# Reordering the prologue of a cross-attention and feed-forward kernel: Q first, batch 0's Q spread without DRAM, later batches prepared one step sooner

## The reference, cut to what matters

```python
Q = heads(layernorm(x) @ w_q.T)        # x: 8 batches x 256 tokens x 128
K = heads(ctx @ w_k.T); V = heads(ctx @ w_v.T)   # 16 heads of width 8
attn = softmax(where(mask, Q @ K.T / sqrt(8), -inf))
x = x + (attn @ V) @ w_o.T
h = silu(layernorm(x) @ w_gate.T) * (layernorm(x) @ w_up.T)    # 384 wide
out = x + h @ w_down.T
```

## Time and profile before

| | |
|---|---|
| median of 3 executions | 182.03 us (181.5 to 182.88) |
| the profiled execution's own time | 182.24 us |
| its span in the trace | 180.4 us |
| prologue, up to the first score matmul | 19.62 us |
| sixteen maxima of batch 0 | 13.03 us |
| steps 0 to 6 | 15.55, 15.67, 16.56, 17.20, 17.19, 16.67, 16.67 us |
| step 7 and the end | 32.24 us |

### The profile page before, as it was taken

The page is one execution under the profiler, slowest core; times in us unless marked ns, Lnnn a source line. Parts: engine busy times, 40 slices in busy tenths (PEclk is TensorE's granted clock), DMA queues, the critical chain, the costliest instruction groups (busy, mean ns, idle before and its releaser), DMA issues.

```text
span 180.4 us, 4294 instructions
## 1 busy us (share of the span) xinstructions
PE 165.1 (91%) x1630; PEld 103.6 (57%) x1630; DVE 134.4 (74%) x315; ACT 109.9 (61%) x231; POOL 63.4 (35%) x108
## 2 busy tenths in 40 slices
PE   5877999998998799999999999999899999999693
PEld 5556655554554346557655765575465546656583
DVE  6844579789499779868986889789978982533763
ACT  4434421985596588847866786677677746866130
POOL 8421655531307741971396058100500050000100
PEclk9996999999999999999999999999999999999999
DMA  4729989188059007803950593069100000100011
GB/s 150 270 64 204 243 144 239 52 219 140 0 145 202 11 8 216 136 0 93 222 79 0 143 198 47 4 187 174 25 2 29 5 0 2 33 2 0 4 60 29
DMA packets 17525, 17.06 MB, mean 95 GB/s; under 512 B 1536, under 2 KB 16128, under 8 KB 16832
## 3 DMA queue, kind: packets, MB, share of 16 engines
q1 hardware_dynamic: 17040, 16.12, 39.0%
q10 hardware_dynamic: 464, 0.67, 1.4%
HBM read 9.24 MB, written 7.34 MB: 92 GB/s over the span
## 4 chain that ended last, share of the span: by engine, by line
PE 68%; DVE 22%; ACT 2%; DMA 2%; issue 2%; ACTq 1%; SPq 1%
PE pv_bank L340 14%; DVE neg_max L818 12%; PE score_bank L280 11%; PE max_bank L297 5%; PE pv_bank L428 5%; PE ffn_bank L405 4%; PE ffn_bank L393 4%; PE ffn_bank L396 3%; PE post_bank L381 2%; DMA ctx_all<-ctxT 2%; PE prep_bank L319 2%; PE post_bank L357 2%; DVE x L896 2%; DVE stats L902 2%; PE prep_bank L311 2%
## 5 line engine op out<-in xcount | busy, mean ns | idle before, releaser
L818 DVE TENSOR_REDUCE neg_max<-max_bank 128x2 f32<-128x512 f32 x128 | 82.0, 684 | 15.6 <-PE max_bank L297 15.2
L613 ACT ACTIVATE probs<-score_bank 128x512 f32<-128x512 f32 x128 | 70.3, 598 | 22.0 <-PE score_bank L280 21.8
L297 PE MATMUL max_bank<-k_ops,q_ops 49*128 49x256 bf16 x256 | 43.2, 273 | 4.0 <-DVE neg_max L818 3.9
L280 PE MATMUL score_bank<-q_ops,k_ops 51*128 51x256 bf16 x256 | 42.8, 273 | 0.6 <-ACT probs L613 0.4
L340 PE MATMUL pv_bank<-probs,v_ops 128*32 128x256 f32 x480 | 32.5, 385 | 0.0
L280 PEld LDWEIGHTS score_bank<-q_ops,k_ops 51*128 51x128 bf16 x256 | 19.3, 94 | 19.5 <-ACT probs L613 9.1
L297 PEld LDWEIGHTS max_bank<-k_ops,q_ops 49*128 49x128 bf16 x256 | 16.7, 94 | 10.9 <-DVE neg_max L818 7.5
L1101 POOL CAST max_parts<-neg_max 128x16 bf16<-128x16 f32 x14 | 2.8, 198 | 54.9 <-DVE neg_max L818 54.9
L340 PEld LDWEIGHTS pv_bank<-probs,v_ops 128*32 128x32 f32 x480 | 13.7, 109 | 9.5 <-issue 4.0
L1108 POOL TENSOR_TENSOR rstd<-var,minus_half 128x2 f32<-128x2 f32 x8 | 5.6, 702 | 32.5 <-DVE var L915 32.5
L428 PE MATMUL pv_bank<-ident_bf 128*128 128x128 bf16 x150 | 14.7, 252 | 1.9 <-POOL ident_bf L1131 1.9
(11 more groups left out here) (139 smaller groups left out, 232.3 us busy)
## 6 DMA issues: line engine op xcount, KB each, us to landing
k_ops<-k_rows SPq DMA_DIRECT2D x7, 384.0 KB, 4.7
q_ops<-q_rows SPq DMA_DIRECT2D x7, 384.0 KB, 6.2
k_rows<-kq_parts SPq DMA_DIRECT2D x8, 192.0 KB, 2.1
q_rows<-kq_parts SPq DMA_DIRECT2D x8, 192.0 KB, 2.2
k_rows<-kq_parts SPq DMA_DIRECT2D x8, 128.0 KB, 2.1
q_rows<-kq_parts SPq DMA_DIRECT2D x8, 128.0 KB, 2.1
out<-y SPq DMA_DIRECT2D x7, 128.0 KB, 2.3
x_all<-x SPq DMA_DIRECT2D x1, 768.0 KB, 6.2
```

What stands on the lines that cost most here:

```text
L280: mm = pe.matmul(score_bank[k % 2][:, t * S:(t + 1) * S], rows(k_ops, b, ROWS)[:, k, t * P:(t + 1) * P], rows(q_ops, b, ROWS)[:, k, :], st ...
L297: mm = pe.matmul(max_bank[k % 2][:, t * S:(t + 1) * S], rows(q_ops, b, MAX_ROWS)[:, k, t * P:(t + 1) * P], rows(k_ops, b, MAX_ROWS)[:, k, ...
L613: act.activation(probs[:, k % RING].rearrange("p t s -> p (t s)"), score_bank[k % 2][:, :], ACT.Exp, scale=SCALE).then_inc(probs_ready, 1)
L818: dve.tensor_reduce(neg_max[:, b % 2, :, k], max_bank[k % 2][:, :].rearrange("p (t s) -> p t s", t=TT), AX.X, ALU.max, negate=True).then_i ...
```

## The change

1. SP's loads: x of batch 0 before ctx of batch 0; x in three more pieces (batch 1, batches 2 and 3, batches 4 to 7), the last issued only after batch 1's K and mask; ctx of batches 2 and 3 with the first loads.
2. Q's chain of batch 0 is moved ahead on PE, ACT and DVE. The fill of the second Q buffer leaves DVE, that of the second K buffer moves back on ACT, behind the prologue; the fills of the V buffers 2 and 3 go from ACT to POOL; the mask is made earlier.
3. Batch 0's Q no longer goes through DRAM: six DMAs, five on SP and one on ACT, copy a part of 128 partitions straight into a block of 8 rows by 16 heads (`spread_q`).
4. K of batch 1 is read back before the last write of batch 1's Q.
5. The preparation (x's statistics, layer norm, K and Q) of batches 4 to 7 is one step sooner, in steps 0 to 3. Steps 0 to 2 have one batch's statistics each and the stage of the sixteen maxima has batch 4's.
6. The numbers of `keep_warm` are changed, and four of the seven in step 0 are gone, two halved.

```diff
-        q_rows = [nc.dram_tensor(f"q_rows{b}", [SPREAD, HEADS * S], BF16, kind="Internal") for b in range(B)]
+        q_rows = {b: nc.dram_tensor(f"q_rows{b}", [SPREAD, HEADS * S], BF16, kind="Internal") for b in range(1, B)}
...
+        def spread_q(eng, part, n):
+
+            first, stride, _ = Q_GROUPS[part]
+            row = DK * (first + stride * n)
+            eng.dma_start(rows(q_ops, 0, SPREAD)[row:row + DK], kq_parts[:, 0, part, S:2 * S]).then_inc(q_direct, 16)
...
+            sp.dma_start(x_all[:, 0], x[:, 0]).then_inc(x_in[0], 16)
             sp.dma_start(ctx_all[:, 0], ctxT[:, 0]).then_inc(ctx_in[0], 16)
-            sp.dma_start(x_all[:, 0], x[:, 0]).then_inc(x_in[0], 16)
             sp.dma_start(x_all[:, 1], x[:, 1]).then_inc(x_in[1], 16)
             sp.dma_start(ctx_all[:, 1], ctxT[:, 1]).then_inc(ctx_in[1], 16)
-            sp.dma_start(x_all[:, 2:B], x[:, 2:B]).then_inc(x_in[2], 16)
+            sp.dma_start(x_all[:, 2:4], x[:, 2:4]).then_inc(x_in[2], 16)
+            sp.dma_start(ctx_all[:, 2:4], ctxT[:, 2:4]).then_inc(ctx_in[2], 16)
...
-            for part, done in enumerate((q_part1, q_part2, q0_part3)):
-                sp.wait_ge(done, 1)
-                to_dram(0, 0, part)
             sp.wait_ge(q_filled[0], 1)
-            sp.wait_ge(q_bounced[0], 16 * PARTS)
-            for g in range(2):
-                half_from_dram(sp, 0, g)
-            sp.dma_start(ctx_all[:, 2:4], ctxT[:, 2:4]).then_inc(ctx_in[2], 16)
+            sp.wait_ge(q_part1, 1)
+            spread_q(sp, 0, 0)
+            spread_q(sp, 0, 1)
+            sp.wait_ge(q_part2, 1)
+            spread_q(sp, 1, 0)
+            spread_q(sp, 1, 1)
+            sp.wait_ge(q0_part3, 1)
+            spread_q(sp, 2, 0)
```

PE, the prologue:

```diff
-            keep_warm(18, pv_bank)
+            keep_warm(30, pv_bank)
             pe.wait_ge(wkq_loaded, 16)
             project_k(0, score_bank[0][:, 0:S]).then_inc(k_proj, 1)
+            keep_warm(8, pv_bank)
+            turn_xn1(0, score_bank[1])
             project_k(1, max_bank[0][:, 0:S]).then_inc(k_proj, 1)
-            keep_warm(16, pv_bank)
-            turn_xn1(0, score_bank[1])
-            keep_warm(6, pv_bank)
             project_q(0, ffn_bank[:, 0:S]).then_inc(q_proj, 1)
             pe.wait_ge(wvo_loaded, 16)
             project_v(0, post_bank)
+            keep_warm(10, pv_bank)
             turn_xn1(1, prep_bank)
-            keep_warm(6, pv_bank)
+            keep_warm(24, pv_bank)
             project_q(1, score_bank[1][:, 0:S]).then_inc(q_proj, 1)
+            keep_warm(20, pv_bank)
             pe.wait_ge(v_ready, 1)
             project_v(1, post_bank)
-            keep_warm(40, pv_bank)
+            keep_warm(30, pv_bank)
```

PE, the sixteen maxima of batch 0 and the steps:

```diff
             for k in range(HEADS):
                 max_head(0, k)
-                keep_warm(4, pv_bank)
-                if k == 3:
+                if k not in (6, 9, 10, 12, 15):
+                    keep_warm(4, pv_bank)
+                if k == 6:
                     turn_xn1(2, prep_bank)
-                if k == 6:
+                if k == 9:
...
-                if k == 14:
+                if k == 15:
                     pe.wait_ge(xn1_t_ready, 4)
                     project_k(3, prep_bank[:, 0:S])
...
-                prep = 1 <= b < B - 3
+                prep = b < B - 4
...
-                    turn_xn1(b + 3, prep_bank)
+                    turn_xn1(b + 4, prep_bank)
...
+                    pe.wait_ge(v_ready, 3)
+                    turn_xn1(4, prep_bank)
...
-                    pe.wait_ge(xn1_t_ready, b + 4)
-                    project_k(b + 3, prep_bank[:, 0:S])
-                    project_q(b + 3, prep_bank[:, S:2 * S]).then_inc(kq_proj, 1)
+                    pe.wait_ge(xn1_t_ready, b + 5)
+                    project_k(b + 4, prep_bank[:, 0:S])
+                    project_q(b + 4, prep_bank[:, S:2 * S]).then_inc(kq_proj, 1)
```

POOL, the prologue and the maxima:

```diff
             fill_v(0)
+            root_of_x(0)
+            pool.wait_ge(xn1_done, 1)
             fill_v(1)
-            root_of_x(0)
             root_of_x(1)
             part3_of_1(k_part2, 0, k1_part3)
-            part3_of_1(q_part2, S, q1_part3)
             root_of_x(2)
             normalise_x(2)
+            part3_of_1(q_part2, S, q1_part3)
             root_of_x(3)
             normalise_x(3)
+            fill_v(2)
+            fill_v(3)
             split_kq(2)
             part3_kq(2)
+            root_of_x(4)
+            normalise_x(4)
```

167 lines of the change are left out of this document (78 added, 89 removed).

## The result

| | before | after |
|---|---|---|
| median | 182.27 us (181.5 to 182.88, 4 runs) | 188.75 us (188.18 to 190.95, 4 runs) |
| profiled execution, its span | 182.24, 180.4 | 190.95, 189.2 |

The ratio is 1.038 (95% interval 1.0285 to 1.0475): the change makes the kernel slower. In this document an execution's clock is the mean of PE's granted clock over its span; the 59 executions of the kernel before that ran beside the experiments lie between 0.969 and 1.00. Ratios are taken over the undisturbed executions of both kernels alone, so where an edit costs the clock in some of its executions, their number stands beside the ratio.

A forecast was written before the change was run, and what follows sets the result against it. Prologue bound by a chain of latencies, maxima by DVE, steps 0 and 1 by DVE with PE, step 4 by PE. -3.4 - 0.4 - 1.5 - 0.7 + 0.3 - 0.5 + 0.2 = -6.0, from 182.24 to 176.2 us (173.9 to 179.6).

The forecast's parts named there:

- Prologue: Stage before the first score matmul: Q in at 13.9, first score matmul at 16.2, 3.4 us less (1.8 to 4.0).
- Rival B: Prologue: six spreads land one behind the other, first score matmul stays at 19.5; 179.5 us in all, chance 0.08.
- Rival C: Step 0: PE's clock falls because most warm-ups are gone, +9 us, so 185.2 in all; chance 0.04.
- ACT has Q: Prologue: ACT has batch 0's Q projection at 8.9 us, or 9.5 if PE's clock is still low.
- PE's own queue: Prologue: PE's queued work, ending in 30 warm-ups, is last and ends at 16.2 us (15.6 to 17.8).
- K's halves: Prologue: read back from 11.0 us (to 11.8), taking 4.1, with the first in at 15.1 (to 16.4).
- Maxima: Sixteen maxima of batch 0: less interruption by preparations, batch 4's statistics added; -0.4 us (0 to -0.8).
- Step 0: Step 0: one batch's statistics and most warm-ups go, so the next step starts 1.5 us sooner (0.5 to 1.8).
- Step 1: Step 1: loses one batch's statistics, but the residual waits for PE's output projection; -0.7 us (-0.3 to -1.1).
- Steps 2 and 4: Step 2 has 0.87 more DVE work, +0.3 us (0 to 0.6); step 4 loses a preparation, -0.5.
- Loads: Feed-forward weights ahead of step 0: first exp 0.9 us late against PE, mostly hidden; +0.2 us (0 to 2.0).
- Rival A: Ahead of step 0: weights or batch 1's Q land late by 2.4 us; price 2.2, 178.4 in all, chance 0.16.

The follow-up runs named there:

- e4: The changed kernel with batch 0's Q through DRAM again and 60 instead of 30 warm-ups ahead of the maxima: 178.62 us, ratio 0.9827 to the kernel before.
- e6: The changed kernel with its spreads, 120 instead of 30 warm-ups ahead of the maxima and twelve more in step 1: 181.63 us, ratio 0.9984.
- m1: A kernel of transfers only: one 64 KB spread into 8 partitions took 3.1 us, six in a row 8.8, six with K's halves beside them 11.2.
- m2: Transfers only, six in a row: into 8 partitions 8.96 us, 16 partitions 6.34, 128 partitions 5.17, 119 partitions 6.36, 8 partitions from two queues 8.89.
- m4: Transfers only, six 64 KB spreads: into blocks of 8 neighbouring partitions 8.50 us, into every sixth partition 5.66, the latter from two queues 4.95.
- e1: The changed kernel with batch 0's Q through DRAM again: 177.6 and 178.28 us at clock 1.00 (ratio 0.980), 182.87 and 184.24 at 0.953 and 0.944.
- e2: The changed kernel with 120 instead of 30 warm-ups ahead of the maxima: 182.62 us, ratio 1.004.
- e8: e4 with step 0's warm-ups as in the kernel before, 32 more: 180.73 us, ratio 0.9947.
- e9: e4 with batch 6's statistics in step 0 instead of step 1: a single execution, step 1 14.76 us against 15.64, no total given.
- e7: e4 with only Q's third part copied directly and 44 warm-ups: median 180.34 us; ratio 0.973 for three of six executions, the others 183.0 to 186.5.

## Why the prediction was wrong

Three versions split the 8.8 us of span, each by subtraction of the row above it, from one profiled execution each:

| step | span | difference | where |
|---|---|---|---|
| before | 180.4 | | |
| e4: all parts but the spreads, PE covered | 176.4 | -4.0 | prologue -2.2, maxima -0.3, step 0 -1.3, step 2 +0.2, step 4 -0.3 |
| e6: with the spreads, PE covered | 179.6 | +3.2 | prologue +3.3, maxima -0.5, step 0 +0.4 |
| after: without the cover and e6's twelve warm-ups | 189.2 | +9.6 | maxima +7.9, step 1 +1.5, prologue +0.2 |

The profiled execution of the kernel before had a clock of 0.991. On e4's chip its executions at 1.00 take 180.3 to 181.0 and e4's take 178.2, so at equal clock e4 gains 2 to 3 us and not 4.0.

**The step that failed** is in *Prologue*: "I take 2.5, near the one of the same size, so Q is in at 13.9". Q was in at 20.75. The 2.5 was the price of one transfer by its size, taken from a write to DRAM. One spread by itself takes 3.1 (m1), six in a row 8.8, and six with K's halves beside them 11.2, near the 11.6 of after. A price for one was used for six that are under way together, and the bound of 16.0 had the same fault. So the prologue, forecast 3.4 shorter, was 1.3 longer.

**What I did not price** is the second half of that step. *Rival B* had the slow landing (19.5 for the first score matmul, measured 20.88), from a rate that it assumed and that no row showed. The number of engines, which it gave as a reason, isn't what limits (m2); that the eight partitions are neighbours is (m4). And it took the idle PE for free: "the prologue gives nothing but 0.1". *Rival C* had the mechanism and nearly the size, +9 for a clock that falls, but looked for it only in step 0, where the warm-ups were removed. The profile before did show it: in the earlier trace rows two matmuls take 1.22 again behind 2.64 us of idle. B's wait of 4.9 triggers C's fall, in the stage where PE has no slack (12.98 busy of 13.03 in the earlier trace rows). B gave 179.5; with C's +9 that is 188.5, and no case stood there. That this sum meets the measured 188.75 is luck in part: C's +9 was worked out for the PE work of step 0, where the lower level cost nothing, and the 7.9 and 1.5 were paid in the maxima and in step 1. The chance of 0.04 on the slower side followed from treating B and C apart.

**Right:** ACT has Q at 8.57 (8.9 forecast), PE's own queue ends at 16.02 (16.2). The last spread was issued at 11.97 (11.4).

*K's halves*, taken at 4.1, needed 6.1 and 7.7 beside the spreads. The first was issued at 10.4, so it landed at about 16.5: 16.2 was just out of reach for K too.

*Maxima*, -0.4: with the clock held -0.1 to -0.8 (e1 12.91, e4 12.70, e2 12.23 against 13.03). Right.

*Step 0*, -1.5: -1.6 in e1, -1.3 in e4. Right, and the warm-ups were most of it: e8 gives 1.38 back with them.

*Step 1*, -0.7: 0.0 (15.63 and 15.64 against 15.67). Wrong in size. It lost one batch's statistics and gained nothing, while the next one taken out gave up to 0.88 (e9). Part of it depends on how step 0 ends: behind e8's long step 0 it takes 15.27. The rest stays open.

*Steps 2 and 4*, +0.3 and -0.5: +0.2 and -0.3. *Loads*: in e4 ACT idled 2.37 for the weights and its first exp came 1.3 behind step 0's first score matmul, against 0.4 in the kernel before: 0.8 late, where 0.9 was forecast. No wait for the weights entered any chain that I read, and step 0 with the clock held took 13.98 to 14.66. Rival A did not occur.

The best version that keeps its clock in all executions is e4: the change with batch 0's Q through DRAM and PE covered until Q has landed, 178.62, 1.7% under the kernel before. Three executions of e7 were about 0.6 faster than e4's best, and its other three lost the clock.

## What to carry to other kernels

Price a group of transfers as a group, and by the partitions that it writes: six of 64 KB into eight neighbouring partitions took 8.5 us where the comb of the same size took 5.7. Price also what runs beside the group: with two reads of 192 KB beside them six took 11.2 instead of 8.8. In this kernel the path through DRAM was faster than the direct one. Whenever a wait of PE gets longer, price what the idle time does to its clock, in the stage behind it and not only in the one that was edited. Rivals that can trigger each other need a case of their own.
